# Layer 3 of a four-layer graph network: one narrow weight block applied to each vector component, in place of three block-diagonal wide ones

## The reference

```python
m1_s, m1_v = _cg_tp(msg_s, msg_v, y0, y1, w1...)      # (E,96), (E,128,3)
a = leaky(m1_s @ W_alpha); a = sum(a * alpha_dot)     # a logit for each head, softmax over dst
val_s = m1_s @ Ws_val
val_v = einsum('ecx,cd->edx', m1_v, Wv_val)           # (128 -> 32) for each component x
val_v = val_v * sigmoid(val_s @ Wg)[..., None]
m2_s, m2_v = _cg_tp(sigmoid(val_s), val_v, y0, y1, w2...)
hs = m2_s @ Ws_vlin                                   # (E, 4 heads, 16)
hv = einsum('ecx,cd->edx', m2_v, Wv_vlin)             # (128 -> 4 heads x 8) for each component x
agg = segment_sum(alpha * concat(hs, hv), dst)
out = node + concat(agg_s @ Wps, agg_v by Wpv)
```

## Time and profile before

| | us |
|---|---|
| median of 3 runs | 14556.21 |
| lowest and highest | 14520.14, 14629.96 |
| the profiled execution | 14520.14 |
| its span, first to last instruction | 14518.4 |

### The profile page before, as it was taken

The page is one execution under the profiler, slowest core; times in us unless marked ns, Lnnn a source line. Parts: engine busy times, 40 slices in busy tenths (PEclk is TensorE's granted clock), DMA queues, the critical chain, the costliest instruction groups (busy, mean ns, idle before and its releaser), DMA issues. The chain is left out here.

```text
span 14518.4 us, 298687 instructions
## 1 busy us (share of the span) xinstructions
PE 11751.5 (81%) x76172; PEld 8152.7 (56%) x76173; DVE 8626.0 (59%) x30542; ACT 5078.7 (35%) x15312; POOL 8651.1 (60%) x13301
## 2 busy tenths in 40 slices
PE   5445542888879999869996897799999999999998
PEld 1000000666645555336664797577777777777776
DVE  6455552899744443133332555677777777777776
ACT  0000000566512222111111000466666666666665
POOL 2777775676657676137775000466666666666665
PEclk9999999999979898655555898799999999999998
DMA  3101110333433335324448774000000000000001
GB/s 139 27 24 27 27 26 11 69 69 68 57 61 74 69 72 65 23 56 82 82 82 55 119 116 72 17 18 18 18 17 18 18 18 17 18 18 18 17 18 19
DMA packets 1123580, 666.64 MB, mean 46 GB/s; under 512 B 711710, under 2 KB 1045491, under 8 KB 1117786
## 3 DMA queue, kind: packets, MB, share of 16 engines
q0 software_dynamic: 257120, 382.51, 15.3%
q1 hardware_dynamic: 850410, 235.44, 9.4%
q10 hardware_dynamic: 15568, 43.25, 0.8%
HBM read 574.19 MB, written 86.47 MB: 46 GB/s over the span
## 5 line engine op out<-in xcount | busy, mean ns | idle before, releaser
L1099 POOL DMA_INDIRECT l2s_node_rows<-node_table,l2s_edge_rows x1216 | 1154.3, 949 | 871.0 <-DMA l2s_edge_rows<-rows_by_src 486.7
L1099 POOL DMA_INDIRECT l1s_node_rows<-node_table,l1s_edge_rows x1216 | 1256.4, 1033 | 648.5 <-issue 320.9
L1184 PE MATMUL l1s_p_outer<-l1s_edge_by_node,l1s_node_rows 128*32 128x64 f32 (+2 forms) x14592 | 1242.6, 274 | 130.6 <-DMA l1s_node_rows<-node_table,l1s_edge_rows 96.0
L448 PE MATMUL rank<-onehot,lower_h 128*128 128x418 f16 x812 | 429.6, 529 | 1021.9 <-DVE onehot L424 958.7
L1184 PE MATMUL l2s_p_outer<-l2s_edge_by_node,l2s_node_rows 128*64 128x40 f32 (+1 forms) x4864 | 1038.8, 345 | 247.9 <-DMA l2s_node_rows<-node_table,l2s_edge_rows 245.7
L731 POOL DMA_INDIRECT l_source_rows<-node_table,l_edge_rows x928 | 949.8, 1023 | 436.6 <-issue 271.7
L1184 PEld LDWEIGHTS l2s_p_outer<-l2s_edge_by_node,l2s_node_rows 128*64 128x64 f32 (+1 forms) x4864 | 839.0, 233 | 638.4 <-issue 412.3
L1184 PEld LDWEIGHTS l1s_p_outer<-l1s_edge_by_node,l1s_node_rows 128*32 128x32 f32 (+2 forms) x14592 | 768.5, 132 | 685.5 <-issue 509.9
L461 POOL DMA_INDIRECT rows_by_src<-row_s,pos_i x812 | 839.7, 1034 | 494.3 <-issue 494.3
L1855 POOL DMA_INDIRECT l_source_rows<-node_table,l_edge_rows x914 | 899.0, 984 | 318.6 <-issue 246.4
L1883 POOL TENSOR_TENSOR l_logits_kept<-l_logits,l_empty_row 128x8 f32<-128x8 f32 x456 | 432.0, 947 | 979.4 <-DVE l_logits L2164 979.4
(11 more groups left out here) (495 smaller groups left out, 32003.1 us busy)
## 6 DMA issues: line engine op xcount, KB each, us to landing
l_xv_by<-h_turned_l SPq DMA_DIRECT2D x300, 128.0 KB
l_source_rows<-node_table,l_edge_rows POOLq DMA_INDIRECT x1842
l_xs_by<-h_turned_l SPq DMA_DIRECT2D x100, 256.0 KB
l_a_by<-sums_turned_l SPq DMA_DIRECT2D x100, 256.0 KB
rows_by_src<-zero_rows ACTq DMA_DIRECT2D x23, 1024.0 KB
l1s_edge_rows<-rows_by_src SPq DMA_DIRECT2D x304, 76.0 KB
l2s_edge_rows<-rows_by_src SPq DMA_DIRECT2D x304, 76.0 KB
l1s_node_rows<-node_table,l1s_edge_rows POOLq DMA_INDIRECT x1216
```

The lines of the kernel that those rows point to most:

```text
L448: nc.tensor.matmul(rank[:, b, 0:BINS], K["lower_h"][:, :], onehot[:, b, :], start=True, stop=False)
L1099: pool.indirect_dma_start(xg[q][:, s, :], None, table, bass.IndirectOffsetOnAxis(ap=pay[q][:, s, S_DST:S_DST + 1].bitcast(U32), axis=0)).t ...
L1184: ins = nc.tensor.matmul(p_o[rows, j % RING, col:col + n], xg[q][:, s, lhs], rhs(eh[q % RING][:, s, :, :]), start=True, stop=True, skip_gr ...
```

## The change

`w_v` and `w_hv` become plain 128x32 tiles, loaded once each. The three matmuls of a component group use the same narrow tile, and each writes its own 32 columns (in `p_h`: 8 columns of each of the four heads, 40 apart) with `start=True, stop=True`. The stationary operands, the number of matmuls, the PSUM layout and all waits stay. In the setup 34 loads become 30, two memsets of 288 columns go, and the three scalings of `w_hv` work on 32 columns.

```diff
-        w_a, w_v = sb("w_a", [P, D]), sb("w_v", [P, 3, 3 * CV])
-        w_hs, w_hv = sb("w_hs", [P, CS]), sb("w_hv", [P, 3, HEADS, 3, AV])
+        w_a, w_v = sb("w_a", [P, D]), sb("w_v", [P, CV])
+        w_hs, w_hv = sb("w_hs", [P, CS]), sb("w_hv", [P, CV])
...
-            n_loads, LOADS = [], 34
+            n_loads, LOADS = [], 30
...
-                    for i in range(3):
-                        load(w_v[:, i, CV * i:CV * (i + 1)], W3("Wv_val"))
-                        load(w_hv[:, i, :, i, :], W3("Wv_vlin").rearrange("f (h c) -> f h c", c=AV))
+                    load(w_v[:, :], W3("Wv_val"))
                     load(wg[:, :], W3("Wg"))
                     load(w_hs[0:MS, :], W3("Ws_vlin"))
+                    load(w_hv[:, :], W3("Wv_vlin"))
...
-                    for t in (wq1, wq2, wp1, wp2, w_a, w_hs, w2s, w_v, w_hv):
-                        nc.vector.memset(t[...], 0.0)
+                    for t in (wq1, wq2, wp1, wp2, w_a, w_hs, w2s):
+                        nc.vector.memset(t[:, :], 0.0)
...
-                    scaled(all_hv(slice(0, P)), w2v[:, 0:1])
+                    scaled(w_hv[:, :], w2v[:, 0:1])
...
-                    scaled(all_hv(slice(0, MS)), 0.5)
-                    scaled(all_hv(slice(MS, P)), 0.5 * r2)
+                    scaled(w_hv[0:MS, :], 0.5)
+                    scaled(w_hv[MS:P, :], 0.5 * r2)
...
                                 for i in range(3):
-                                    ins = nc.tensor.matmul(p_a[:, s, D:256], f_t[s][:, (i + 1) * P:(i + 2) * P], w_v[:, i, :], start=i == 0, stop=i == 2)
+                                    ins = nc.tensor.matmul(p_a[:, s, D + CV * i:D + CV * (i + 1)], f_t[s][:, (i + 1) * P:(i + 2) * P], w_v[:, :], start=True, stop=True)
...
                                 for i in range(3):
-                                    ins = nc.tensor.matmul(heads(s)[:, :, AS:AS + 3 * AV], g_t[s][:, (i + 1) * P:(i + 2) * P], w_hv[:, i, :, :, :].rearrange("p h j c -> p h (j c)"), start=i == 0, stop=i == 2)
+                                    ins = nc.tensor.matmul(heads(s)[:, :, AS + AV * i:AS + AV * (i + 1)], g_t[s][:, (i + 1) * P:(i + 2) * P], split(w_hv[:, :], AV), start=True, stop=True)
```

More of the change, by code:

```diff
@@ L1731, in _ @@
                     scaled = lambda ap, f: v.done(nc.vector.tensor_scalar(ap, ap, f, None, ALU.mult))
-                    all_hv = lambda rows: w_hv[rows, :, :, :, :].rearrange("p i h j c -> p (i h j c)")
                     r2, r3 = 2.0 ** -0.5, 3.0 ** -0.5
```

## The result

| | us |
|---|---|
| changed kernel, median of 4 runs | 15217.93 (15167.18 to 15285.00) |
| kernel before, median of 4 runs beside it | 14593.08 (14520.14 to 14658.81) |
| ratio, with its 95% interval | 1.040 (1.035 to 1.046) |
| profiled execution of the changed kernel | 15279.55, span 15277.8 |

The change makes the kernel slower, by 625 us between the medians. The executions of the changed kernel fall into a faster and a slower state, and the ratio, 4.0% or some 590 us, is of the faster ones alone. The forecast was slower by 1,394 us, with a range from 14,700 to 18,000 us. The direction is as forecast, the size is less than half of it.

What follows compares the result with a forecast made beforehand. PE's record queue and a DVE-to-POOL chain beside it close each 11.43 us loop turn; 14,520 + 1,396 (clock) - 4 (setup) = 15,912 us, forecast as 15,950 since run medians lie 36 us higher; range 14,700 to 18,000 us.

Steps and rivals of the forecast that it cites:

- Narrower records come no sooner: L1961 and L1986, 24 records per turn: 32 columns keep the 110 to 114 ns spacing, so no time gained.
- The gap by column count: Skill's N/2.4 + 2.5 ns per isolated matmul, about 42 ns at 96 columns; set aside for the rows' 110 ns.
- The setup: Before the layers: four fewer loads (2.5 us), two fewer memsets, three smaller scalings; together about 4 us saved.
- The clock falls in the loop because the part around the pause is thinned: Layer 3 loop, L1968 to L1917: streamed columns drop from 1,808 to 1,040, so the clock falls; 1,396 us more, chance 0.80.
- The rival that the clock holds: Layer 3 loop stays at 1.00, leaving setup and at most 0.05 us per turn: 14,529 us; chance 0.14, including falls costing under 1%.
- The low turn: Loop turn wholly at 1.2 GHz: PE alone binds it, 10.5 x 1.88 = 19.8 us, 8.4 us longer than 11.43.
- Half of the loop at the low clock: Loop time split evenly between both clock levels: mean turn 14.5 us, 3.06 us more, 1,396 us over 456 turns.
- the middle between two ways of recovering: Clock recovers at once behind dense 128-column records (layer 2), or not for 12.5 us behind L1184's records (layer 1); half taken.
- behind the narrower records of L1184: Layer 1, from 4486.5: clock stays at 0.50 for 12.5 us although PE is fully busy, records taken as narrower.
- near bound: Loop falls as short as layer 2's, 1.5 us lost each, one in every fourth turn: 170 us.
- POOL's wait as a limit at L1994: Turn's end: POOL's L1893 finishes 0.15 us before L1994 starts, so a small PE gain from L1911 on would be taken back.

Runs made afterwards that it cites:

- the kernel with the wide gather: Kernel before, wide weights kept, with only the one-hot gather at L1978 streaming 124 columns instead of 4; 14225.02 us against 14590.41, ratio 0.977.

## Why the forecast was right, and where it was wrong

- **Narrower records come no sooner: right.** Costed at 0 from the spacing of 110 to 114 ns in the earlier trace rows; measured 111 ns at 32 columns, and the kernel with only `w_v` narrow is unchanged within 0.4%. The gap by column count that the prediction took from the Trainium skill ("TensorE: Matmul & The Clock Gate", "Back-to-back issue gap"), which gives it for an isolated matmul, would have meant a gain; no run shows one.
- **The setup: right.** From the first memset to the first operation behind the loads it took 9076.50 - 9054.72 = 21.8 us, now 9224.60 - 9206.24 = 18.4, and to the copy into `w_a` behind the scalings 23.8, now 20.0. The difference at the end is 3.8 us. The forecast was 4.

The rows for that, DVE in order of time, the kernel before and the changed one:

```profile
9054.72 0.65 DVE L1718 MEMSET l_wq<- 128x320 f32 x2 [1.33 <-PEq L92]
...
9076.50 0.06 DVE L1730 MEMSET l_loads_seen<- 1x1 f32 x1
```

```profile
9206.24 0.65 DVE L1717 MEMSET l_wq<- 128x320 f32 x2 [1.33 <-PEq L92]
...
9224.60 0.06 DVE L1729 MEMSET l_loads_seen<- 1x1 f32 x1
```

- **The clock falls in the loop because the part around the pause is thinned: right, and shown.** Narrowing L1961, away from the pause, makes no fall. Narrowing L1986, behind it, makes 145. Adding columns in that part, with turn and pause as they were, leaves 18 or 36% of the low time. And all falls begin just behind that part. The pause's own part isn't shown: nearly all falls of the changed kernel follow a pause of 0.3 us or more, but no kernel has the thin part without one. The rival that the clock holds is refuted. It had leant on pauses of 0.7 us being shorter than those seen before other falls, and beside it stood the Trainium skill's rule ("TensorE: Matmul & The Clock Gate", "Why this matters for your kernels") that only long pauses of PE matter. Here the clock falls with pauses of at most 0.77 us, so that rule isn't enough.
- **The low turn: nearly right.** 10.5 x 1.88 = 19.8 us forecast, 18.69 measured. With half of the time low that alone makes the mean turn 2 / (1/11.42 + 1/18.69) = 14.18 and not 14.5 us: about 145 us too many.
- **Half of the loop at the low clock: the step that failed.** It was chosen as the middle between two ways of recovering, with no row of the loop behind it, and one of the two was misread, as the row below shows. Measured is 30.5%. With the measured turns that gives 1 / (0.695/11.42 + 0.305/18.69) = 12.96 us, 1.22 less than 14.18: about 555 us too many. It is the bulk of the error.

PE in order of time in layer 1, the kernel before, just ahead of the low stretch from 4486.5 on:

```profile
4484.63 3.29 PE L1184 MATMUL l1s_p_outer<-l1s_edge_by_node,l1s_node_rows 128*64 128x128 f32 x35 [0.95 <-issue]
```

The prediction has the clock stay low there "behind the narrower records of L1184". They are 128 columns wide, as wide as the dense ones of layer 2; the narrow ones (40 columns) are those of layer 2's first half. So the row doesn't say that narrow records delay the recovery. The pause ahead of that fall was 0.95 us too, not 1.3: in the stretch of 1.30 us PE was still busy for 0.38.

- **Short falls are partly hidden: not in the sum.** 12.96 is not 12.77 either. A turn with 3.41 us at the low clock is only 12.20 - 11.42 = 0.78 us longer, where 3.41 x (1 - 11.42/18.69) = 1.33 us would follow from the low turn. The trace shows where the rest goes. PE is idle 0.92 us in a turn without low clock, 0.20 us in one with 3.4 us of it, and not at all with 6.8 us. PE's own work is 11.42 - 0.92 = 10.50 us at full clock and 18.69 at the low one, so 3.41 us at the low clock put it back by 3.41 x (1 - 10.50/18.69) = 1.49 us, and 0.72 us of pauses take that up: 0.77 us, as measured. (The prediction's near bound priced such a fall at 1.5 us; that is PE's share without the pauses.) Over 456 turns it is 0.19 x 456 = 87 us.
- 1,396 - 145 - 555 - 87 = 609 us, the loop's measured gain in time.
- **POOL's wait as a limit at L1994: right as a remark, not followed up.** The prediction named the 0.15 us between POOL's L1893 and L1994 as what would take back a gain on PE. It didn't ask why POOL's chain ends so late. Its first operation, 0.96 us long, was mostly waiting for DVE, and there lay 2.5% that neither kernel has.

## What to carry to other kernels

Zeros that TensorE multiplies cost no time as long as the spacing of the records doesn't follow their columns: before they are cut, the spacing of narrow records in the trace tells whether cutting brings any time, and the granted clock tells what they may be holding up, above all next to a pause that recurs. Two edits of that kind have to be tried together as well as apart, since one that costs nothing alone can lengthen the low stretches that the other brings. And one operation with two durations in the groups (0.22 and 0.96 us for 128x8) is worth a look at what runs beside it, even where its engine looks idle.

## What the runs showed of the hardware that was not expected

- Columns can be had free and be worth something: in the kernel with the wide gather, four records of 4 columns widened to 124 cost about 0.07 us per turn on PE (12010.59 - 12010.08 = 0.51 us from L1978 to L1984, before 0.44).
- A run of DVE operations on two SBUF operands kept a 128x8 operation of POOL out for 0.7 us, over several of them and not for one. The Trainium skill ("SBUF — State Buffer", "SBUF: two separate sides") has the two engines share ports under an exclusive lock that is held for one instruction. Who waits for whom agrees with that; the length does not: POOL's 0.96 us outlast the longest single DVE operation beside it (0.34 us).
- It seems to go the other way too, though no run tests it. DVE's L2134 takes 0.35 us with none of POOL's tensor operations beside it (8 turns of the kernel before), 0.46 us with two (224 turns), and 0.77 to 0.85 us with three or four of them (223 turns). In the kernel with the wide gather two others lie beside it in 442 of 456 turns, and it takes 0.385 us. Groups by line and shape, DVE, 9400 to 14000, the kernel before and then that one:

```profile
L2134 DVE TENSOR_TENSOR l_dot_parts<-l_weighted_v,l_edge_rows 128x192 f32<-128x192 f32 x403 | 253.3, 629 | 0.0
```

```profile
L2134 DVE TENSOR_TENSOR l_dot_parts<-l_weighted_v,l_edge_rows 128x192 f32<-128x192 f32 x429 | 165.2, 385 | 0.0
```

- The clock of a stretch that nobody touched (layer 1) had a mean of 0.79 to 0.90 in the profiled executions compared here. Between the first two profiles it makes 142 us, a quarter of what the change did.
